# A fused two-level kernel: where the second level scales its last third and adds its bias

## The reference, cut to what matters

```python
x = x + L0_ffn(L0_cond(x, cond))        # four modulated convolutions, then gated low-rank adapters
x = x + L1_ffn(L1_cond(x, cond))        # four modulated convolutions, then an int4 product
# L1_ffn: q = the int4 values of qweight as float32, (1024, 1024)
W = scales[None, :] * q - zeros[None, :]
out = x @ W + bias
```

## Time and profile before

| | us |
|---|---|
| median of 3 runs | 897.18 |
| lowest and highest | 896.91, 898.37 |
| the profiled execution | 897.48 |
| its span, first to last instruction | 895.7 |
| TensorE busy | 886.0 (99%) |
| VectorE busy | 594.2 (66%) |
| ScalarE busy | 496.2 (55%) |
| GpSimd busy | 90.6 (10%) |

### The profile page before, as it was taken

How to read it: one execution, slowest core, us unless ns; L and a number is a source line. 1 busy time by engine, 2 the same in 40 slices (tenths; PEclk the granted TensorE clock), 3 DMA queues, 4 the chain that set the end, 5 groups by cost and what they waited for, 6 DMA issues and landing times.

```text
span 895.7 us, 15997 instructions
## 1 busy us (share of the span) xinstructions
PE 886.0 (99%) x5318; PEld 822.9 (92%) x5318; DVE 594.2 (66%) x1327; ACT 496.2 (55%) x977; POOL 90.6 (10%) x113
## 2 busy tenths in 40 slices
PE   9999999999999999999999999999999999999998
PEld 8889899899899898998998998988899999999988
DVE  8896455455365464464454565578599998999975
ACT  5965445455355255264354434378577767777650
POOL 0000000000000000000000030220221112211121
PEclk9999999999999999999999999999999999999999
DMA  8702101101102011011011111325122122212221
GB/s 292 254 0 72 70 20 50 51 22 68 47 23 70 26 44 70 23 47 70 23 47 70 54 62 48 64 65 173 48 95 71 71 90 97 94 70 72 71 94 71
DMA packets 33134, 64.32 MB, mean 72 GB/s; under 512 B 11728, under 2 KB 14032, under 8 KB 33104
## 3 DMA queue, kind: packets, MB, share of 16 engines
q1 hardware_dynamic: 24032, 30.90, 11.1%
q0 software_dynamic: 9072, 33.03, 9.7%
HBM read 47.14 MB, written 16.78 MB: 71 GB/s over the span
## 4 chain that ended last, share of the span: by engine, by line
PE 91%; DVE 4%; ACT 3%; issue 1%; DMA 1%; SPq 0%; DVEq 0%; ACTq 0%
PE conv_ps L184 6%; PE conv_ps L186 6%; PE conv_ps L185 6%; PE fold_ps L730 6%; PE prod_ps L1031 6%; PE prod_ps L1029 6%; PE prod_ps L1030 6%; PE prod_ps L996 5%; PE prod_ps L998 5%; PE prod_ps L997 5%; PE prod_ps L1105 4%; PE prod_ps L1104 4%; PE fold_ps L695 3%; PE turn_ps L950 3%; PE turn_ps L998 2%; PE turn_ps L997 2%
## 5 line engine op out<-in xcount | busy, mean ns | idle before, releaser
L839 ACT ACTIVATE data<-conv_ps,bias,scale 64x256 f32<-64x256 f32 x200 | 101.1, 556 | 0.7
L1029 PE MATMUL prod_ps<-b_hi,xt 128*128 128x512 f32 x240 | 93.6, 390 | 0.0
L1031 PE MATMUL prod_ps<-b_hi,xt 128*128 128x512 f32 x240 | 93.5, 390 | 0.0
L1030 PE MATMUL prod_ps<-b_lo,xt 128*128 128x512 f32 x240 | 93.5, 389 | 0.0
L956 ACT ACTIVATE xt<-turn_ps 128x512 fp32r<-128x512 f32 x32 | 17.4, 594 | 136.9 <-PE turn_ps L950 136.9
L1089 DVE SCALAR_TENSOR_TENSOR res<-prod_ps,norm,res 128x512 f32<-128x512 f32 x32 | 23.9, 750 | 87.8 <-PE prod_ps L1031 86.7
L996 PE MATMUL prod_ps<-a_hi,xt 128*128 128x384 f32 x240 | 81.2, 338 | 0.0
L998 PE MATMUL prod_ps<-a_hi,xt 128*128 128x384 f32 x240 | 81.1, 338 | 0.0
L997 PE MATMUL prod_ps<-a_lo,xt 128*128 128x384 f32 x240 | 81.0, 338 | 0.0
L1104 PE MATMUL prod_ps<-quant,xt_hi 128*128 128x342 f32 x256 | 80.7, 319 | 0.0
L1105 PE MATMUL prod_ps<-quant,xt_lo 128*128 128x342 f32 x256 | 80.5, 320 | 0.0
(11 more groups left out here) (314 smaller groups left out, 2590.7 us busy)
## 6 DMA issues: line engine op xcount, KB each, us to landing
x_in<-in_x SPq DMA_DIRECT2D x64, 128.0 KB, 2.7
res<-in_x POOLq DMA_DIRECT2D x16, 512.0 KB, 3.5
x_after_first<-res POOLq DMA_DIRECT2D x16, 512.0 KB, 2.9
x_in<-x_after_first SPq DMA_DIRECT2D x64, 128.0 KB, 2.7
res<-x_after_first POOLq DMA_DIRECT2D x16, 512.0 KB, 3.5
out_x<-res POOLq DMA_DIRECT2D x15, 512.0 KB, 3.0
a_raw<-in_adapter_in SPq DMA_DIRECT2D x8, 544.0 KB, 8.9
b_raw<-in_adapter_out SPq DMA_DIRECT2D x8, 512.0 KB, 7.9
```

The costliest lines, as they stand in the source:

```text
L839: last = nc.scalar.activation(data[rows, first:first + HALF], conv_ps[a][rows, parity:H:2], ACT.Identity, bias=at(bias1, c, a, bufs)[rows] ...
L1029: nc.tensor.matmul(prod_ps[n][:, :], bufs.xt_hi[:, k, :], bufs.b_hi[:, k, cols], start=(k == 0), stop=False)
L1030: nc.tensor.matmul(prod_ps[n][:, :], bufs.xt_hi[:, k, :], bufs.b_lo[:, k, cols], start=False, stop=False)
L1031: last = nc.tensor.matmul(prod_ps[n][:, :], bufs.xt_lo[:, k, :], bufs.b_hi[:, k, cols], start=False, stop=(k == KT - 1))
```

## The change

Three things change, all in level 1 from pair 16 on.

- VectorE scales the last third of the product (L1120) ahead of the join of sample 0, where it stood behind it. The addition L1133 stays behind that join, except in the last step (28), where it goes behind the join of sample 1 and the turn of pair 29. The new argument `whole` tells the addition apart from the third.
- GpSimd adds the bias two pairs ahead, where it was one: two biases before its loop, and at pair `f` that of pair `f + 2`.
- That bias stands right behind the issue of pair `f`'s store, and ahead of the wait for the store and of the next load. It stood behind the load.

```diff
--- before.py
+++ after.py
@@ -1105,7 +1105,7 @@
                 last = nc.tensor.matmul(out, bufs.xt_lo[:, k, :], bufs.quant[:, k, cols], start=False, stop=(k == KT - 1))
             last.then_inc(S.out_done, 1)
 
-        def dve_second_residual(v, f, bufs, apart=False, last=False, parts=(0, 1, 2)):
+        def dve_second_residual(v, f, bufs, apart=False, last=False, parts=(0, 1, 2), whole=True):
             g = f - NPAIR
             thirds = [slice(max(n * QCOLS, ONES) - ONES, (n + 1) * QCOLS - ONES) for n in range(3)]
             if 0 in parts:
@@ -1127,7 +1127,7 @@
                 if last:
                     v.wait_ge(S.x1_ready, evicted(f, n + 1))
                     nc.vector.tensor_tensor(bufs.res[:, cols], bufs.res[:, cols], bufs.scaled[:, cols], ALU.add).then_inc(S.y_ready, 1)
-            if not last and 2 in parts:
+            if not last and whole:
                 v.wait_ge(S.zeros_added, g + 1)
                 v.wait_ge(S.x1_ready, evicted(f, 3))
                 nc.vector.tensor_tensor(bufs.res[:, :], bufs.res[:, :], bufs.scaled[:, :], ALU.add).then_inc(S.y_ready, 1)
@@ -1365,18 +1365,20 @@
                 load_residual(f, f % SLOTS)
             pool.wait_ge(S.consts_loaded, 16 * 3)
             pool.wait_ge(S.edges_done, 2)
-            add_bias(FIRST % SLOTS, 1)
+            for n in range(2):
+                add_bias((FIRST + n) % SLOTS, 1)
             with pool.Fori(0, (END - FIRST - 1 - AHEAD) // SLOTS) as n:
                 for j in range(SLOTS):
                     f = SLOTS * n + (FIRST + j)
                     slot = (FIRST + j) % SLOTS
-                    add_bias((slot + 1) % SLOTS, n + (1 if j + 1 < SLOTS else 2))
                     store_output(f, slot)
+                    add_bias((slot + 2) % SLOTS, n + (1 if j + 2 < SLOTS else 2))
                     pool.wait_ge(S.y_stored, 16 * (f - NPAIR) + 16)
                     load_residual(f + SLOTS, slot)
             for f in range(END - 1 - AHEAD, END - 1):
-                add_bias((f + 1) % SLOTS, (f + 1 - FIRST) // SLOTS + 1)
                 store_output(f, f % SLOTS)
+                if f + 2 < END:
+                    add_bias((f + 2) % SLOTS, (f + 2 - FIRST) // SLOTS + 1)
                 if f + SLOTS < END:
                     pool.wait_ge(S.y_stored, 16 * (f - NPAIR) + 16)
                     load_residual(f + SLOTS, f % SLOTS)
@@ -1992,15 +1994,19 @@
                 dve_differences(v, c, 1, bufs)
                 for a in range(2):
                     dve_parity_lo(v, c, a, bufs)
-                dve_second_residual(v, i, bufs, parts=(0, 1))
+                dve_second_residual(v, i, bufs, parts=(0, 1), whole=False)
                 if left:
                     dve_filter_sums(v, c + 1, bufs)
                     split(c + 1, bufs)
+                dve_second_residual(v, i, bufs, parts=(2,), whole=False)
                 dve_join(v, c, 0, bufs)
-                dve_second_residual(v, i, bufs, parts=(2,))
                 if not left:
                     dve_turn(v, i + 1, slot(i + 1))
+                else:
+                    dve_second_residual(v, i, bufs, parts=())
                 dve_join(v, c, 1, bufs)
+                if not left:
+                    dve_second_residual(v, i, bufs, parts=())
                 if left > 1:
                     dve_fold_start(v, c + 2, bufs)
 
```

## The result

| | before | changed |
|---|---|---|
| median (runs) | 897.53 us (4) | 903.55 us (4) |
| lowest and highest | 896.91, 898.37 | 903.20, 903.73 |
| ratio, 95% interval | | 1.0066 [1.0049, 1.0083] |
| span of the profiled execution | 895.7 | 901.9 |

The account below looks back on a forecast made before the run. TensorE, busy 99% of the span, was taken as the bound. 11 stalls of 0.85 us (9.35) less 1.8 and 1.8 gave +5.75 on 897.48: 903.2, median 0.3 lower, 902.9 us; range 893.0 to 904.6.

Parts of the forecast that it names:

- the likeliest case: Level 1 from pair 16: the bias behind the store holds `v_lo` in all pairs; 902.9 us, 901.0 to 905.0, chance 0.56.
- What was to be had (3.6 us): TensorE's stalls in the changed stretch, all to be won: 1.8 us at L730 and 1.8 us in step 28.
- the two stalls of the earlier trace: TensorE's fold L730 waiting 7 times for `r_lo`, 1.8 us together; pair 29's transposes in step 28 waiting 1.8 us.
- Who gets the lock: Bias against two-SBUF-input VectorE instructions: straight behind a DMA issue, the bias claims it about 0.14 us after that issue's start.
- the second rival: Behind the store, the bias does not get the lock ahead of `v_lo`; all gains stay, 893.6 us, chance 0.24.
- The "one bias" of the earlier trace: The bias that is first behind the loop's branch; it lost to `sum_lo`, which took 0.69 us, the bias 2.74.
- The stall a pair (0.85): TensorE at L695 and L1104, late by 0.66, then 0.8 plus about 0.05 for the semaphore: 0.85 us in 11 pairs.
- Pair 16: Ahead of the loop: second `v_lo`, 0.17 us after the store, is held too; an 11th stall of 0.85 us.
- The third: Rival: only the second `v_lo` is held; stall 0.5 us in 10 pairs, none in pair 16; 898.6 us, chance 0.11.
- The fourth: Rival: the hold comes only in one slot of three, 4 x 0.85 - 3.6 = -0.2 us; 897.0 us, chance 0.09.

Follow-up runs that it names:

- hold_turn: The whole change, but GpSimd waits between the store and the bias until ScalarE has written the next pair's first `xt_hi`; 893.50 us against 897.00 before.
- dve_only: VectorE's half of the change alone, with GpSimd's list as in the kernel before; 894.62 us against 897.00 before.
- apart: The whole change, but in the loop a one-column fill and a wait for its semaphore stand between store and bias; 893.78 us against 897.47 before.
- pool_only: GpSimd's half of the change alone, with VectorE's list as in the kernel before; 908.40 us against 897.00 before.

## Why the prediction was right

**What the range says.** Little. 893.0 to 904.6 takes in a gain of 4 us and a loss of 7, since the rival without a hold had a chance of 0.24 and was taken in; 903.55 lies near its upper end. What was right is the likeliest case, at a chance of 0.56, with its time (902.9) and the waits that it named.

**What was to be had (3.6 us).** Right. With `v_lo` out of the way the stores lie 3.7 us closer together (`hold_turn`), and the two stalls of the earlier trace rows are what has gone. In `dve_only` only part of the second was won (0.7 of its 1.8 us stayed, 2.6 won in all): there the chain of VectorE is still late by the bias.

**Who gets the lock.** Right, and this decided the sign. The hold was forecast from two instructions that lost 0.14 and 0.32 behind a load's issue; the first `v_lo`, 0.24 behind a store's by the sum, measured 0.25 and lost. That a store hands over as a load does was the open point of the second rival, and it does; no row before the run showed it. `hold_turn` and `apart` show that the hold comes with the bias standing straight behind. The "one bias" of the earlier trace rows is three in the trace, each time behind the loop's branch back (686.59, 742.61, 798.63), with `sum_lo` 0.20 ahead of the record and not held. The branch must be taken: at the loop's end, where a compare stands there too but doesn't jump, `sum_lo` 0.24 behind the load's issue was held:

```profile
854.12 3.27 DVE L170 TENSOR_TENSOR sum_lo<-whole,sum_hi 128x512 fp32r<-128x512 f32 x1
```

**The stall a pair (0.85).** Right in size. Ten stores of the loop make it plain: they lie 19.34 us apart (664.56 to 838.58 is nine), where `hold_turn` has 18.48 (662.25 to 828.55), so 0.86 a pair. The parts differ a little. L695 is late by 0.59 and not 0.66, and L1104 by 0.73 in all and not 0.8. No row showed the 0.05 for a semaphore; what follows L1104 is 0.10, as its second matmul starts 0.26 behind the first and not 0.16. The errors nearly cancel.

**Pair 16.** The one term that was mis-sized. I charged the same 0.85. There TensorE comes to L695 sooner: without a wait it would start 2.2 us behind the first `v_lo`, in the loop 2.7 (684.16 to 686.90), and `v_lo` is held about as long in both (3.39 and 3.27). VectorE, GpSimd and TensorE of the changed kernel:

```profile
645.35 3.39 DVE L681 SCALAR_TENSOR_TENSOR v_lo<-down_T,scale,v_hi 128x192 fp32r<-128x192 f32 x2
```

```profile
645.52 0.58 POOL L1362 DMA_DIRECT2D out_x<-res  x1 [14.45 <-DVE res L1133]
646.12 2.39 POOL L1358 TENSOR_TENSOR res<-res,bias 128x1024 f32<-128x1024 f32 x1
```

```profile
647.31 0.40 PE L186 MATMUL conv_ps<-x_hi,w_lo 128*128 128x512 f32 x1
648.79 0.44 PE L695 MATMUL fold_ps<-v_hi,fold_hi 128*128 128x384 f32 x1 [1.08 <-DVE v_lo L681]
```

L695 starts 1.48 behind its predecessor, 1.25 more than 0.23, and L1104 and slower first matmuls add some 0.25. The stores give 1.50: the first two lie 19.04 apart, in `hold_turn` 17.54. The forecast had said that each wait stays under 1 us; this one did not. The second `v_lo` was the held one, as forecast. With it the sum is 9 x 0.86 + 0.74 (the last pair, by the stores) + 1.50 - 3.69 = 6.29, and 6.27 was measured. The forecast's 5.75 lacks the 0.65 by which this pair was charged too little; the gains were 0.1 larger than its 3.6.

**Rivals.** The second (no hold, 893.6) is what `apart` and `hold_turn` make of the change, at 893.8 and 893.5; it took one more wait in GpSimd's list. The third (only the second `v_lo` held, cheap) is what happens in `pool_only`, where it cost 0.82 at L695 and not 0.5 in all, since the store comes later there. The fourth fell: 11 waits of 11.

## What to carry to other kernels

Before an engine's work is moved "beside a DMA", look at what the other engine that shares its way to SBUF does in the next three microseconds, and at who waits for that. A hold moved off an instruction that cost TensorE 1.8 us in all (`sum_lo`) onto one that cost it 10 (`v_lo`, just ahead of `xt_lo`) is a loss though nothing was added. A held instruction doesn't show in a busy share, only in its own duration. And a wait on a semaphore that stands for "the other engine is past its sensitive place" cost nothing here, as the moved bias had slack.

## What the runs showed of the hardware

A GpSimd addition of two SBUF tiles (2.4 us) and a VectorE instruction with two SBUF inputs exclude each other, and who gets in first can't be read from the recorded starts.

- Straight behind a DMA issue the addition wins early: VectorE instructions that started between 0.14 and 0.32 us behind that issue's start, and 0.23 to 0.44 ahead of the addition's record, took 2.5 to 2.7 us longer. In `pool_only` one that started 0.10 ahead of the issue did not.
- With a wait between that had nothing left to wait for, the same `v_lo` at the same 0.16 was not held (`hold_turn`, pair 16). With a small instruction and a wait between, one 0.16 ahead of the record was not held (`apart`). Nor was one 0.20 ahead behind a taken branch. At the loop's end, where the branch was not taken, one 0.31 ahead was held. Why a wait or a taken branch lets VectorE in is not shown.
- Eight GpSimd fills that read nothing did not hold a `v_lo` that ran beside them (0.41 us).

TensorE's first matmul behind a wait had its successor 0.28 behind it (687.49 to 687.77) where 0.18 is the distance in the kernel before. It was 0.25 to 0.28 in all 11 places, so each such wait cost a tenth of a microsecond more than its length.
